# Self attention of layer 0: the output projection computed transposed, with the weights stationary, and turned back one turn later

## The reference, cut to what matters

```
def _L0_attn_ref(residual, Wq, Wk, Wv, Wo, bq, bk, bv, bo):
    q = einsum('bsd,hda->bhsa', residual, Wq) + bq     # k and v alike
    scores = einsum('bhsa,bhta->bhst', q, k) / sqrt(64)
    pattern = softmax(where(causal, scores, -100000.0), axis=-1)
    z = einsum('bhst,bhta->bsha', pattern, v)
    return einsum('bsha,had->bsd', z, Wo) + bo         # the part that is changed
x = x + _L0_attn_ref(layernorm(x), ...)
```

## Time and profile before

| | us |
|---|---|
| median of 3 runs | 3454.67 |
| the profiled execution's own time | 3452.34 |
| its span, first to last instruction | 3450.6 |
| TensorE busy (share of the span) | 3254.7 (94%) |
| VectorE / ScalarE / GpSimd busy | 1887.5 (55%) / 1646.8 (48%) / 783.8 (23%) |
| mean granted TensorE clock | 0.974 |
| this sublayer, from the first matmul group to the last add | about 13 to 602 |

### The profile page before, as it was taken

One profiled execution on the slowest core, in us unless ns is written; L12 is line 12 of the kernel. 1 busy time (PEld: TensorE's weight loads), 2 busy tenths in 40 slices (PEclk: granted clock), 3 DMA queues, 4 the chain that ended last, 5 costly groups with the idle time before them and its releaser, 6 DMA issues. The chain is left out here.

```text
span 3450.6 us, 76147 instructions
## 1 busy us (share of the span) xinstructions
PE 3254.7 (94%) x24554; PEld 2422.0 (70%) x24555; DVE 1887.5 (55%) x5145; ACT 1646.8 (48%) x4614; POOL 783.8 (23%) x854
## 2 busy tenths in 40 slices
PE   8999999899999989899998989999999999998992
PEld 6777776566666656677776766777777777766871
DVE  4655555577777756122222664666666666663433
ACT  4555555566666611122222326666666666652220
POOL 1000000000000000333332110132332332336774
PEclk9999999899999989999999999999999999999996
DMA  8500000400000051211112100010000000025784
GB/s 274 151 0 0 0 0 0 157 9 11 11 11 11 5 161 43 77 30 31 30 29 46 52 0 5 16 43 21 18 14 11 15 13 12 13 81 141 203 221 137
DMA packets 136407, 181.28 MB, mean 53 GB/s; under 512 B 36156, under 2 KB 108601, under 8 KB 135308
## 3 DMA queue, kind: packets, MB, share of 16 engines
q1 hardware_dynamic: 84112, 133.96, 12.6%
q0 software_dynamic: 45760, 26.67, 4.8%
q10 hardware_dynamic: 6460, 19.66, 1.5%
HBM read 116.11 MB, written 103.61 MB: 64 GB/s over the span
## 5 line engine op out<-in xcount | busy, mean ns | idle before, releaser
L1269 DVE TENSOR_REDUCE e_nmx<-PS 128x1 f32<-128x361 f32 x416 | 221.3, 532 | 343.4 <-PE PS L1117 337.5
L1622 ACT ACTIVATE b_p<-PS,b_nmx 100x361 f32<-100x361 f32 x512 | 267.1, 568 | 148.4 <-DVE b_nmx L1704 148.4
L1117 PE MATMUL PS<-e_cT,e_qT 128*128 128x361 f32 x832 | 333.4, 483 | 0.0
L893 POOL DMA_INDIRECT slot_rows<-r_row,r_rows_now x256 | 256.7, 1003 | 336.7 <-DVE e_p L1276 290.2
L1221 ACT ACTIVATE e_pT<-PS 121x384 f32<-121x384 f32 (+1 forms) x416 | 199.0, 479 | 220.9 <-PE PS L1124 220.8
L2637 PE MATMUL PS<-c_wgu,c_tile_xT 128*128 x912 | 291.2, 463 | 1.4 <-ACT c_tile_xT L2692 1.4
L1704 DVE TENSOR_REDUCE b_nmx<-PS 100x1 f32<-100x361 f32 x512 | 243.5, 525 | 44.6 <-PE PS L1468 44.6
L1124 PEld LDWEIGHTS PS<-ident,e_p 128*121 128x121 f32 x1248 | 198.0, 184 | 96.2 <-ACT e_pT L1221 0.4
L1226 ACT ACTIVATE e_p<-PS,e_nmx 128x361 f32<-128x361 f32 x416 | 232.4, 559 | 36.3 <-DVE e_nmx L1269 36.2
L1475 PEld LDWEIGHTS PS<-ident,b_p 100*121 100x121 f32 x1536 | 188.5, 185 | 61.2 <-ACT b_pT L1606 31.0
L1475 PE MATMUL PS<-ident,b_p 100*121 100x100 f32 x1536 | 223.5, 280 | 6.5 <-ACT b_pT L1606 4.4
(11 more groups left out here) (338 smaller groups left out, 6462.9 us busy)
## 6 DMA issues: line engine op xcount, KB each, us to landing
f_w<-in_f_W SPq DMA_DIRECT2D x64, 384.0 KB, 3.7
slot_rows<-a_empty SPq DMA_DIRECT2D x1, 21504.0 KB, 65.3
f_xg<-slot_rows SPq DMA_DIRECT2D x64, 336.0 KB, 3.9
c_wgu<-in_c_GU ACTq DMA_DIRECT2D x8, 1408.0 KB, 16.6
sum<-X SPq DMA_DIRECT2D x2, 3200.0 KB, 57.0
f_sums<-sum SPq DMA_DIRECT2D x16, 400.0 KB
b_cT<-in_ctx_T SPq DMA_DIRECT2D x32, 181.5 KB, 2.3
e_cT<-in_ctx_T SPq DMA_DIRECT2D x32, 181.5 KB, 2.3
```

Of the source, the lines that this page charges most:

```text
L893: pool.indirect_dma_start(out=self.rows, in_=self.row[:, u, :], in_offset=None, out_offset=bass.IndirectOffsetOnAxis(ap=self.rows_now[:, u ...
L1117: sr.fill_done(pe.matmul(sr.at(f"s{m}", ROWS, CTX), qT[:, at:at + ROWS], cT[:, u, 0:CTX], start=True, stop=True), f"s{m}")
L1269: dve.tensor_reduce(nmx[:, m:m + 1], sr.at(f"s{m}", ROWS, CTX), AX.X, ALU.max, negate=True).then_inc(max_ready, 1)
L1622: sr.move_done(act.activation(p[:, g % 2, a, 0:CTX], sr.at(f"s{g}{a}", S, CTX), ACT.Exp, bias=nmx[:, g, a:a + 1]), f"s{g}{a}")
```

## The change

The two projections of a turn become one, `out(i)`, behind the stage-3 work where `out(1)` stood. It keeps Wo stationary (128 x 128 pieces) and moves the attention output of both sequences, 2 x 100 = 200 columns; the result is z transposed, 128 channels x 2 x 200, in one PSUM bank. ScalarE copies it into a new tile a_zT (`move_turned`) at the head of the next turn. In stage 1 of the next turn, where `out(0)` stood, TensorE transposes the four 128 x 100 pieces back into one bank (`turn_back`), and VectorE adds both sequences at once (100 x 512). Turn 0 is now written out before the loop, since it has nothing to turn back, and behind turn 15 there is one more `move_turned`, `turn_back` (into bank 0) and `add`.

```
-        oT = sb("a_oT", [128, 2, T, S])
+        oT, zT = sb("a_oT", [128, T, 2, S]), sb("a_zT", [128, KC, 2, S])
...
-        mr = Ring(k, 5, 3).plan(["xT", "q0", "k0", "q1", "k1", "q2", "k2", "y0", "q3", "k3", "v00", "v01",
-                                 "v10", "v11", "y1"]).ends(TURNS, ["y0", "y1"])
+        mr = Ring(k, 5, 3).plan(["xT", "q0", "k0", "q1", "k1", "q2", "k2", "y", "q3", "k3", "v00", "v01",
+                                 "v10", "v11", "z"]).ends(TURNS, ["y", "z"])
+        mr.done_in({"y": 1})
+        last_y = Banks(k, 0, 1).plan(["y"])
...
-                def out(u, i):
-                    ob.wait_moved(pe, i, f"o{2 * u + 1}")
-                    mr.wait_free(pe, f"y{u}", i)
-                    for t in range(T):
-                        last = pe.matmul(mr.at(f"y{u}", S, D), oT[:, u, t, :], wo[:, t, :],
-                                         start=(t == 0), stop=(t == T - 1))
+                def out(i):
+                    ob.wait_moved(pe, i, f"o{HALVES - 1}")
+                    mr.wait_free(pe, "z", i)
+                    for c in range(KC):
+                        for t in range(T):
+                            last = pe.matmul(mr.at("z", 128, KC, 2 * S)[:, c, :], wo[:, t, c * 128:(c + 1) * 128],
+                                             oT[:, t].rearrange("p u s -> p (u s)"), start=(t == 0), stop=(t == T - 1))
+                def turn_back(banks, i, t):
+                    mr.wait_moved(pe, i, "z")
+                    banks.wait_free(pe, "y", t)
+                    for u in range(2):
+                        for c in range(KC):
+                            last = pe.transpose(banks.at("y", S, 2, KC, 128)[:, u, c, :], zT[:, c, u, :], k.ident[:])
...
-                        if this and n == 1:
-                            out(0, i)
+                        if prev and n == 1:
+                            turn_back(mr, i - 1, i - 1)
...
                         if this and n == 3:
-                            out(1, i)
+                            out(i)
...
+                def move_turned(i):
+                    mr.wait_full(act, "z", i)
+                    mr.move_done(act.activation(zT[:], mr.at("z", 128, KC, 2, S), ACT.Copy), "z")
...
+                        if prev and n == 0:
+                            move_turned(i - 1)
...
-                        if this and n == 1:
-                            add(0, i)
+                        if prev and n == 1:
+                            add(mr, i - 1, i - 1)
...
-                        if this and n == 3:
-                            add(1, i)
```

More of the change, by code:

```diff
@@ L320, in self_attention @@
         ob = Banks(k, 4, 1).plan([f"o{h}" for h in range(HALVES)])
-        mr = Ring(k, 5, 3).plan(["xT", "q0", "k0", "q1", "k1", "q2", "k2", "y0", "q3", "k3", "v00", "v01",
-                                 "v10", "v11", "y1"]).ends(TURNS, ["y0", "y1"])
+        mr = Ring(k, 5, 3).plan(["xT", "q0", "k0", "q1", "k1", "q2", "k2", "y", "q3", "k3", "v00", "v01",
+                                 "v10", "v11", "z"]).ends(TURNS, ["y", "z"])
+        mr.done_in({"y": 1})
+        sr.done(TURNS)
+        last_y = Banks(k, 0, 1).plan(["y"])
+        last_y.done(1)
         def ahead(n, by, i, this, nxt):
@@ L437, in weigh, with turn @@
                     ob.fill_done(last, f"o{h}")
-                def out(u, i):
-                    ob.wait_moved(pe, i, f"o{2 * u + 1}")
-                    mr.wait_free(pe, f"y{u}", i)
-                    for t in range(T):
-                        last = pe.matmul(mr.at(f"y{u}", S, D), oT[:, u, t, :], wo[:, t, :],
-                                         start=(t == 0), stop=(t == T - 1))
-                    mr.fill_done(last, f"y{u}")
-                def turn(i, this, nxt):
+                def out(i):
[5 more added lines that the diff above has]
+                                             oT[:, t].rearrange("p u s -> p (u s)"), start=(t == 0), stop=(t == T - 1))
+                    mr.fill_done(last, "z")
+                def turn_back(banks, i, t):
[4 more added lines that the diff above has]
+                            last = pe.transpose(banks.at("y", S, 2, KC, 128)[:, u, c, :], zT[:, c, u, :], k.ident[:])
+                    banks.fill_done(last, "y")
+                def turn(i, this, nxt, prev):
                     for n in range(HALVES):
@@ L476, in turn @@
                             project("k", 0, i)
[L477 to L478 removed]
+                        if prev and n == 1:
+                            turn_back(mr, i - 1, i - 1)
                         elif n == 1:
[L480 removed]
+                            mr.pass_over_in(pe, i, "y")
                         if nxt and n == 2:
@@ L486, in turn @@
                         if this and n == 3:
-                            out(1, i)
+                            out(i)
                         elif n == 3:
-                            mr.pass_over(pe, "y1")
+                            mr.pass_over(pe, "z")
                         if w_at:
@@ L494, in turn @@
                             project("k", 1, i)
-                turn(-1, False, True)
+                turn(-1, False, True, False)
                 pe.wait_ge(wo_loaded, 16)
-                with pe.Fori(0, TURNS - 1) as i:
-                    turn(i, True, True)
-                turn(TURNS - 1, True, False)
+                turn(0, True, True, False)
+                with pe.Fori(1, TURNS - 1) as i:
+                    turn(i, True, True, True)
+                turn(TURNS - 1, True, False, True)
+                turn_back(last_y, TURNS - 1, 0)
             @block.scalar
@@ L528, in move_out, with turn @@
                     ob.wait_full(act, f"o{h}", t)
-                    ob.move_done(act.activation(oT[:, u, half * TH:(half + 1) * TH, :], ob.at(f"o{h}", 128, TH, S),
+                    ob.move_done(act.activation(oT[:, half * TH:(half + 1) * TH, u, :], ob.at(f"o{h}", 128, TH, S),
                                                 ACT.Copy), f"o{h}")
-                def turn(i, this, nxt):
+                def move_turned(i):
+                    mr.wait_full(act, "z", i)
+                    mr.move_done(act.activation(zT[:], mr.at("z", 128, KC, 2, S), ACT.Copy), "z")
+                def turn(i, this, nxt, prev):
                     for n in range(HALVES):
                         at, w_at = ahead(n, AHEAD, i, this, nxt), ahead(n, WEIGHED, i, this, nxt)
+                        if prev and n == 0:
+                            move_turned(i - 1)
                         if this and n in (0, 2, 3):
@@ L564, in _ @@
                 act.wait_ge(bqk_loaded, 32)
[L565 to L568, removed]
+                turn(-1, False, True, False)
+                turn(0, True, True, False)
+                with act.Fori(1, TURNS - 1) as i:
+                    turn(i, True, True, True)
+                turn(TURNS - 1, True, False, True)
+                move_turned(TURNS - 1)
             @block.vector
@@ L598, in divide, with add @@
                                       ALU.mult).then_inc(scaled, 1)
[L600 to L605, removed]
+                def add(banks, i, t):
+                    dve.wait_ge(biased, i * 2 + 2)
+                    banks.wait_full(dve, "y", t)
+                    at = bass.ds(i * 2, 2)
+                    banks.move_done(dve.tensor_tensor(X[:, at, :], X[:, at, :], banks.at("y", S, 2, D), ALU.add), "y")
                 def norm(t):
@@ L647, in _ @@
                 dve.wait_ge(bq_scaled, 1)
[L648 to L652, removed]
+                turn(-1, False, True, False)
+                turn(0, True, True, False)
+                with dve.Fori(1, TURNS - 1) as i:
+                    turn(i, True, True, True)
+                turn(TURNS - 1, True, False, True)
+                add(last_y, TURNS - 1, 0)
         tr.done(TURNS)
```

## The result

The changed kernel takes 3461.74 us, the median of 14 runs (3455.25 to 3469.13), beside 3453.85 for the kernel before (14 runs). The ratio is 1.0026, 95% interval 1.0019 to 1.0034: slower by about 9 us. The interval lies clear of 1, and its lower end is next to the 0.2% (6.9 us) under which the prediction saw no change that could be told. The forecast had been 3455 within 3445 to 3463. The profiled execution has a span of 3457.6 us against 3450.6.

What follows compares the result with a forecast made beforehand. TensorE's work was taken to bound the loop while its inputs come early. With -1.8 us in the loop and +3.8 at the end, +2.0 on the profiled 3452.34, the forecast was 3455 us, 8 in 10 within 3445 to 3463.

Steps and rivals of the forecast that it cites:

- the forecast case: Whole kernel: 3455 us, bounds 3451 to 3463, a difference under 0.2% not being told from none; chance 0.71.
- the case slower by over 0.2%: Whole kernel slower by over 6.9 us: falling clock, half of the slow-pass rival and the forecast's upper end; chance 0.17.
- TensorE's work bounds the loop.: Loop: TensorE is busy 35.73 of 35.73 us a turn, so its work sets the time while its inputs come early.
- The projection.: Stage 3 and stage 1: z 5.47 us replaces 7.10, transposes add 0.56, so TensorE's work falls 1.07 us a turn.
- Rival B: out(i) in stage 3: passes take 181 ns, z 5.80 us, total 3459.6, or 3463 with a slow clock; chance 0.14.
- The new wait.: Stage 1, before the weighing of half 2: TensorE waits 0.95 us a turn for ScalarE's a_pT, covering the transposes.
- the net of -0.12 us a turn: Loop: stage 1 starts the weighing 2.04 us earlier, stage 3 loses 1.92; -1.8 us over 15 turns.
- The other waits of the loop at nothing.: Loop: a_sm in stage 2 stays 0.5 us early, VectorE's longer add and ScalarE's z copy cost nothing.
- The end.: Turn 15 and after: exposed z, copy, transposes and add cost +2.3 at full clock, +3.8 with +1.5 for low clock.
- the 7.5 and the 12 that were named as signs: Turn 15: last z to the last add's end should take 7.5 us, or up to 12 with a low clock.
- Rival A: Stage 1 of the loop: no wait, TensorE keeps its whole 1.07 us a turn, total 3439 us; chance 0.12.
- Rival C: Loop: the new pause lowers the clock every turn, 3.4 us each, +51 in all, total 3505 us; chance 0.03.

Runs made afterwards that it cites:

- reordered kernels: Changed kernel, both a_pT transposes and copies earlier, keys moved last, norm applied in stage 2: ratio 0.9966 to the kernel before; with turn 15 the old way 0.9931.
- kernel with the exchange: Changed kernel with ScalarE's second copy of a_pT put ahead of the keys in stage 1: ratio 1.0007 to the kernel before.

## Why the prediction was right, and where its sizes were off

The measured time lies in the range, at its upper end; the forecast case had given no measurable change, and the case slower by over 0.2% a chance of 0.17. So the mechanism was right and two sizes were off, both towards slower; that the range still held them is owed to its width, and to a chip on which the kernel before came out at 3453.85 (beside the later experiments the same kernel took 3485 and 3487 us). What the prediction says of the change is the difference. The steps, in their order:

- *TensorE's work bounds the loop.* Right for the kernel before, and by the reordered kernels for the changed one too.
- *The projection.* z was put at 5.47 between 5.33 and 5.80 and measured 5.54, the transposes at 0.56 (0.53 where nothing waits behind them, 225.16 to 225.69). Rival B, 181 ns a pass, is out: (5.54 - 0.14) / 32 is 169 ns. The sign that was named for it, a period of 35.9, was nearly met by 35.85 all the same, so that sign could not tell it from a longer wait; the length of z does. The Trainium skill ("TensorE: Matmul & The Clock Gate", "LDWEIGHTS (loading the stationary operand)") has a load cost its columns / 1.2 ns, an estimate of 107 ns for 128 columns. That it stays hidden under a pass agrees with these 169 ns.
- *The new wait.* Its place, its cause and the sentence that it covers the transposes were right, and the doubled transposes show it. (That ScalarE starts on the exponents when its first copy of a_pT is done, and not at the end of the maximum, changed no term.) Its size was off: 1.08 instead of 0.95. I had taken 0.08 us from the end of ScalarE's copy to the start of the weighing. In the loop it is 0.25 (236.85 + 0.49 = 237.34 to 237.59), and the same in the kernel with the exchange (230.93 to 231.18). I had it from waits like that of turn 15 (596.80), where ScalarE has nothing behind the copy; that this is the difference is a guess. These 0.17 and the 0.07 of z are the whole error: the net of -0.12 us a turn became +0.12, so the sum's loop term was wrong by 3.6 us: +1.8 (15 x 0.12) instead of -1.8.
- *The other waits of the loop at nothing.* Right for the changed kernel. The place that I named as next, a_sm in stage 2, is where the exchanged kernel gave 0.07 back.
- *The end.* Put at +3.8 between +2.3 and +7.6, measured +6.8. By its parts: the transposes of half 3 came 1.03 earlier (1.1 forecast); from them to the last out it took 1.30 more, which the sum did not have, since they and the weighing run at the low clock too (1.55 and 1.60 us); z to its copy 8.67 against 3.73 + 1.92 for the larger group + 1.5 for the clock = 7.15; copy, transposes and add 2.00 against the old add's 0.42 (1.86 forecast). The mis-sized term is the clock: these 1.30 and 1.52 us are nearly all of the 3.0 that the end came out over the forecast. From the start of the last z to the end of the last add it is 10.67 us, between the 7.5 and the 12 that were named as signs. The extra matmuls of the later experiment give 4.3 us of the 6.8 back.
- *Rival A* is out as a forecast, and it is what the change does once the chain is shorter. *Rival C*, a clock that falls in every turn, is out: 1.08 us of pause a turn, and the windows show 1.00. With a pause of 1.52 us (out(0) moved) the clock did fall in three of the 15 turns, at 1.6 us a fall and not the 3.4 that C had put on it. The Trainium skill (same page, "A second HAM failure mode: psum-queue depth-cycling") tells of short idle times between matmul groups that make the clock swing; with 1.08 us in every turn this trace does not show it, with 1.52 us it does in some turns.

## What to carry to other kernels

When an engine is busy 100% of a loop, taking work from it only pays up to the slack of the tightest chain that waits in its queue: read that slack at the place from which the work is taken, not over the turn. Here moving 1.9 us of matmuls from one stage to another cost more than 1.1 us less work brought, and reordering the same work on TensorE, ScalarE and VectorE brought all of it back. Work that is put off by a turn comes out exposed behind the last one, and if the engine has pauses there, it can run at half the clock, as z did here for 6 us; the last turn is worth its own, plainer form.

## What the runs showed of the hardware

From the end of a ScalarE copy to the start of the TensorE group that waited for it it is 0.25 us where ScalarE goes on with the next instruction (237.34 to 237.59), and about 0.1 us where it has none (596.70 to 596.80 in the kernel before); whether that is the reason is not shown. In turn 15 of the kernel before the low clock ended at about 593, after 5.5 us in which TensorE had worked without a pause (587.45 on). In the changed kernel, where it works and pauses by turns from 588.92 on, the low clock lasted from 589 to 606 and ended only under the unbroken z. With most of the pauses filled it did not fall at all in that turn. Inside the loop a pause of 1.08 us in every turn never lowered it, and a pause of 1.52 us did in three turns of 15.
